# First cross attention: scores and maxima in one ring of seven PSUM banks, maxima over 512 columns, one bank for the sums

## The reference

```python
def _L0_xattn_ref(qkv, y):          # qkv: layernorm(x), (1, 256, 512); y: ctx_2048, (1, 4096, 512)
    bs, width, length = qkv.shape
    ch = width // 16                # 16 heads of 16 channels
    q = qkv.reshape(bs * 16, ch, length)
    k = v = y.reshape(bs * 16, ch, -1)          # 8192 keys a head
    scale = 1.0 / math.sqrt(math.sqrt(ch))
    weight = jnp.einsum('bct,bcs->bts', q * scale, k * scale)
    weight = jax.nn.softmax(weight.astype(jnp.float32), axis=-1)
    a = jnp.einsum('bts,bcs->bct', weight, v)
    return a.reshape(bs, -1, length)
```

## Time and profile before

| | us |
|---|---|
| median of 3 runs | 1421.54 (1421.36 to 1424.01) |
| span of the profiled execution | 1419.4 |
| first pre-score to the end of the stage | about 20 to 685 |
| stretch 325.32 to 642.54: TensorE, VectorE, ScalarE busy | 317.22, 313.66, 283.53 |
| whole span: TensorE, VectorE, ScalarE busy | 1368.0, 1153.8, 940.2 |

### The profile page before, as it was taken

The page is one execution under the profiler, slowest core; times in us unless marked ns, Lnnn a source line. Parts: engine busy times, 40 slices in busy tenths (PEclk is TensorE's granted clock), DMA queues, the critical chain, the costliest instruction groups (busy, mean ns, idle before and its releaser), DMA issues. The chain is left out here.

```text
span 1419.4 us, 27290 instructions
## 1 busy us (share of the span) xinstructions
PE 1368.0 (96%) x10665; PEld 832.0 (59%) x10665; DVE 1153.8 (81%) x1680; ACT 940.2 (66%) x1765; POOL 138.5 (10%) x171
## 2 busy tenths in 40 slices
PE   3999999999999999999898999999989989999998
PEld 2433333333333333333457999999978864567997
DVE  5999999999999999998477766666657756887665
ACT  1588888888888888889275555555434631785553
POOL 4122221211222221111000000000000000000000
PEclk9999999999999999999999999999999999999999
DMA  7545555565354554455202854555528524203751
GB/s 179 139 100 122 141 131 139 145 156 118 100 124 100 126 118 98 91 84 83 90 1 106 326 179 177 180 185 194 195 86 344 238 82 156 67 1 92 206 189 38
DMA packets 63569, 192.54 MB, mean 136 GB/s; under 512 B 32872, under 2 KB 33296, under 8 KB 51280
## 3 DMA queue, kind: packets, MB, share of 16 engines
q1 hardware_dynamic: 63264, 190.80, 47.4%
q10 hardware_dynamic: 192, 0.20, 0.1%
HBM read 165.72 MB, written 21.83 MB: 132 GB/s over the span
## 5 line engine op out<-in xcount | busy, mean ns | idle before, releaser
L530 DVE TENSOR_REDUCE pm<-bank 128x1 f32<-128x1024 f32 x512 | 621.0, 1221 | 15.9 <-PE bank L611 10.2
L589 ACT ACTIVATE probs<-bank 128x512 f32<-128x512 f32 x1024 | 554.3, 598 | 98.6 <-PE bank L630 92.9
L611 PE MATMUL bank<-kst,qst 48*128 48x512 f32 x1024 | 371.0, 452 | 21.7 <-DMA qst<-qsplit 20.0
L630 PE MATMUL bank<-qst,kst 52*128 52x512 f32 (+1 forms) x1024 | 372.4, 448 | 2.4 <-DMA qst<-nscratch 1.0
L647 PE MATMUL bank<-probs,vext 128*32 128x256 f32 x3968 | 316.7, 391 | 0.0
L630 PEld LDWEIGHTS bank<-qst,kst 52*128 52x128 f32 (+1 forms) x1024 | 153.0, 185 | 211.9 <-ACT probs L589 182.2
L1378 PE MATMUL bank<-e_xhi,e_hi 128*128 128x256 f32 (+1 forms) x768 | 217.4, 283 | 0.5 <-DVE e_xlo L1438 0.5
L1378 PE MATMUL bank<-e_xhi,e_lo 128*128 128x256 f32 (+1 forms) x768 | 217.2, 283 | 0.0
L1378 PE MATMUL bank<-e_xlo,e_hi 128*128 128x256 f32 (+1 forms) x768 | 217.2, 283 | 0.0
L647 PEld LDWEIGHTS bank<-probs,vext 128*32 128x32 f32 x3968 | 78.1, 108 | 181.1 <-ACT probs L589 91.5
L611 PEld LDWEIGHTS bank<-kst,qst 48*128 48x128 f32 x1024 | 149.8, 186 | 29.3 <-DMA qst<-qsplit 20.0
(11 more groups left out here) (233 smaller groups left out, 1515.6 us busy)
## 6 DMA issues: line engine op xcount, KB each, us to landing
raw<-wall SPq DMA_DIRECT2D x43, 1536.0 KB, 6.6
kst<-kscratch SPq DMA_DIRECT2D x192, 128.0 KB, 4.4
kscratch<-ksplit SPq DMA_DIRECT2D x15, 1024.0 KB, 4.7
kraw<-ctx_rows SPq DMA_DIRECT2D x16, 512.0 KB, 6.1
vraw<-ctx_vt SPq DMA_DIRECT2D x16, 512.0 KB, 7.2
ctxT<-ctxT SPq DMA_DIRECT2D x8, 1024.0 KB, 11.8
nat<-ctx_chunks SPq DMA_DIRECT2D x6, 1024.0 KB, 22.0
weights<-wscratch SPq DMA_DIRECT2D x16, 256.0 KB, 3.4
```

What stands on the lines that cost most here:

```text
L530: nc.vector.tensor_reduce(pm[:, h % 2, r % 4, c:c + 1], bank[:, 2 * (r % 2):2 * (r % 2) + 2, :], AX.XY, ALU.max).then_inc(pre_reduced, 1)
L589: nc.scalar.activation(probs[:, (XST * k + n) % PR, :], bank[:, S_BANK[k][n], :], ACT.Exp, scale=XSCALE).then_inc(probs_ready, 1)
L611: ins = nc.tensor.matmul(bank[:, 2 * (r % 2) + j, :], qst[64 * j:64 * j + KR, h, tt * P:tt * P + P], kst[64 * j:64 * j + KR, h % 2, c * 51 ...
L630: nc.tensor.matmul(bank[:, S_BANK[k][n], :], kst[64 * j:64 * j + rows, h % 2, m * P:m * P + P], qst[64 * j:64 * j + rows, h, :], start=Tru ...
```

## The change

Scores and pre-scores share banks 0 to 6. Slot 2s of the ring is score s, slot 2s + 1 the pre-score that is issued with it, and slot i takes bank i mod 7. So score s waits for the maximum of the pre-score issued with score s - 4, and a pre-score issued with score s for the exponential of score s - 3. The first 48 pre-scores (AHEAD, 24 steps instead of 23 ahead of the first score) still come in pairs in banks 0 to 5 with one maximum over 1024 columns; all others are reduced one by one over 512 columns, so `pm` has twice the places. The last 48 scores, which have no pre-scores beside them, use the five banks LATE_RING. The sums have bank 7 in all rounds: the first sums of each round wait for `o_copied` of the round before. The order of work within a step is as before; tiles are numbered with an offset of two, and the three half groups of sums left at the start of the last round stand in one piece.

```diff
-LAGP = 7
-PVLAG = 2
-FIRST_V = LAGP + 1 + PVLAG
-V_SCORE = 2 * (FIRST_V - LAGP) + 2
-VLAG = 2
...
+ITEMS = XN * XST
+AHEAD = XST + XP
+RING = 7
+STEP = 2
+V_BANK = 7
+V_STEP = 3
+VLAG = 2
+LATE = ITEMS - AHEAD
+LATE_RING = (6, 0, 1, 4, 5)
+PM = 8
...
+def maxima(p):
+    return p // 2 if p <= AHEAD else p - AHEAD // 2
+
+
+def score_bank(s):
+    return 2 * s % RING if s < LATE else LATE_RING[(s - LATE) % len(LATE_RING)]
+
+
+def pre_bank(p):
+    return p % 6 if p < AHEAD else (2 * (p - AHEAD) + 1) % RING
...
+            def tile_max(p):
+
+                dve.wait_ge(pre_scores, maxima(p) + 1)
+                nc.vector.tensor_reduce(max_at(p, 1), bank[:, pre_bank(p), :], AX.X, ALU.max).then_inc(pre_reduced, 1)
...
-                    if n == V_SCORE - 3 and k > 0:
+                    if k > 0 and n == (V_STEP * STEP - 1 if k < XN - 1 else 3):
                         copy_o(k - 1)
...
+                if 6 <= p < AHEAD and p % 2 == 0:
+                    pe.wait_ge(pre_reduced, maxima(p) - 2)
+                elif p >= AHEAD + 3:
+                    pe.wait_ge(probs_ready, p - AHEAD - 2)
...
+                if s < 3:
+                    pe.wait_ge(pre_reduced, maxima(AHEAD) - 2 + s)
+                elif 4 <= s < LATE + 4:
+                    tile_free(s + AHEAD - 4)
+                if LATE <= s < LATE + 4:
+                    pe.wait_ge(probs_ready, s - 3)
+                elif s > LATE + 4:
+                    pe.wait_ge(probs_ready, s - 4)
...
+            def pv(k, q, lo, hi):
+                if lo == 0:
+                    pe.wait_ge(probs_ready, XST * k + 4 * q + 4)
+                    if q == 0 and k % NS == 0:
+                        pe.wait_ge(v_ready, k // NS + 1)
+                    if q == 0 and k > 0:
                         pe.wait_ge(o_copied, k)
...
+            for i in range(AHEAD // 2):
+                pre(2 * i)
+                pre(2 * i + 1)
+                if i >= FIRST_BUSY:
                     first_busy(3)
             pe.wait_ge(const_set, 4)
+            done = 0
             for k in range(XN - 1):
...
+                for i, (first, size) in enumerate(STEPS):
+                    for n in range(first, first + size):
+                        s = XST * k + n
+                        score(s)
+                        if s < LATE:
+                            pre(s + AHEAD)
...
-            last = XN - 1
-            pe.wait_ge(pre_reduced, XP * XN)
-            for i in range(LAGP):
-                for e in range(2):
-                    late_score(last, 2 * i + e)
-                late_values(last, i)
+            last = XST * (XN - 1)
+            rest = D * XG * (XN - 1)
             for q in range(XG + VLAG):
```

More of the change, by code:

```diff
@@ L40 @@
 Q_ROWS = [(0, 0), (XC, 0), (2 * XC, 1)]
-LAGP = 7
-PVLAG = 2
-FIRST_V = LAGP + 1 + PVLAG
-V_SCORE = 2 * (FIRST_V - LAGP) + 2
-VLAG = 2
 FIRST_BUSY = 4
 DLAG = 3
[L49 to L67, removed]
+ITEMS = XN * XST
[8 more added lines that the diff above has]
+PM = 8
+SIZES = [STEP] * (XST // STEP)
+STEPS = [(sum(SIZES[:i]), n) for i, n in enumerate(SIZES)]
+def maxima(p):
[4 more added lines that the diff above has]
+    return p % 6 if p < AHEAD else (2 * (p - AHEAD) + 1) % RING
 class Count:
@@ L570, in copy_o @@
                     act.wait_ge(o_stored[h % 2], h // 2 * 16)
-                nc.scalar.copy(osb[:, 0 if half == 0 else 1 + h % 2, :], bank[:, V_BANK[k], :]).then_inc(o_copied, 1)
+                nc.scalar.copy(osb[:, 0 if half == 0 else 1 + h % 2, :], bank[:, V_BANK, :]).then_inc(o_copied, 1)
             act.wait_ge(g.ident_ready, 2)
@@ new lines, in score @@
+                if LATE <= s < LATE + 4:
+                    pe.wait_ge(probs_ready, s - 3)
+                elif s > LATE + 4:
+                    pe.wait_ge(probs_ready, s - 4)
+                nc.tensor.matmul(bank[:, score_bank(s), :], kst[64 * j:64 * j + rows, h % 2, m * P:m * P + P],
+                                 qst[64 * j:64 * j + rows, h, :], start=True, stop=True).then_inc(scores, 1)
+            def pv(k, q, lo, hi):
[4 more added lines that the diff above has]
+                    if q == 0 and k > 0:
+                        pe.wait_ge(o_copied, k)
@@ L645, in pv @@
                 for e in range(4):
                     n = XST * k + 4 * q + e
-                    ins = nc.tensor.matmul(bank[32 * e:32 * e + 32, V_BANK[k], cols], vext[:, k // NS % 2, chunk(n % XT), :], probs[:, n % PR, cols],
-                                           start=q == 0 and half == 0, stop=q == XG - 1 and half == 1)
-                if half == 1:
+                    ins = nc.tensor.matmul(bank[32 * e:32 * e + 32, V_BANK, lo:hi], vext[:, k // NS % 2, chunk(n % XT), :], probs[:, n % PR, lo:hi],
+                                           start=q == 0 and lo == 0, stop=q == XG - 1 and hi == D)
@@ L650, in pv @@
+                if hi == D:
                     ins.then_inc(pv_done, 1)
[L652 to L655, removed]
-                    ins = nc.tensor.matmul(bank[32 * e:32 * e + 32, V_BANK[k], :], vext[:, k // NS % 2, chunk(n % XT), :], probs[:, n % PR, :],
-                                           start=q == 0, stop=q == XG - 1)
-                ins.then_inc(pv_done, 1)
-            def late_score(k, n):
-                s = n - 2 * LAGP
-                if s >= 0:
-                    score(k, s)
-                elif k > 0:
-                    score(k - 1, XST + s)
```

113 lines of the change are left out of this document (47 added, 66 removed).

## The result

The changed kernel takes 1439.07 us, the median of four runs (1433.76 to 1443.58), the kernel before 1421.49 beside it: 1.0112 times as long, 95% interval [1.0079, 1.0145]. In a second comparison five runs gave 1439.82 (1434.74 to 1441.07), 1.0123 times [1.0106, 1.0140]. So it is slower, as forecast, but by 17.6 us and not by 5.6, and outside the range given (1419.5 to 1431).

What follows compares the result with a forecast made beforehand. The prediction took TensorE to bound the rounds, at 1.24 us a step. Its terms 7.3 + 0.3 - 1.7 - 0.3 gave +5.6 us, so a median of 1427.1 us, range 1419.5 to 1431.

Steps and rivals of the forecast that it cites:

- Part 1: VectorE in the rounds: maxima over 512 columns start 0.60 us apart, a round 19.5 us against TensorE's 19.82; cost 0.
- the cover that the forecast had: VectorE's 0.3 us to spare in each round, 19.5 us against 19.82 of TensorE.
- Rival (a): VectorE becomes the bound in the rounds, from 0.617 us a maximum: 1440 at 0.63, 1496 at 0.69; chance 0.08.
- Part 2: One ring of seven banks in the rounds: nothing waits, a step stays at 1.24 us with waits on all four loads.
- Rival (b): Waits on all loads shorten some 488 steps by 0.01 us each: -4.9, so 1422.2, no change; chance 0.11.
- Part 3: New sums wait for ScalarE's copy, 0.245 us in each of 30 rounds: +7.3; a step of 1.23 becomes 1.24: +0.3.
- Rival (c): No stall, the copy being over when sums come: 1419.8, or 1414.9 with shorter steps; chance 0.12, 0.07 of it with those.
- Parts 4 and 5: End of pre-scores: no drain, eight light steps of 1.00 us, -1.7; last round: earlier copy, sums at 5.7 us, -0.3.
- Part 6: Start: first score still waits for a DMA until 48.2, TensorE stands about 2 us, clock effect taken as 0.
- The signs named: Page after: sums idle about 0.24 us 30 to 31 times, rounds 20.07 apart, first score at 48.2, no end wait.

Runs made afterwards that it cites:

- a_swap: Changed kernel's 512-column maxima, work order and end, but the banks of the kernel before, with the sums' bank changing each round: 1421.58 us, 0.9997 times before.
- b_one_bank: Kernel before with one bank for the sums of all rounds, the first sums awaiting the copy, and nothing else of the change: 1433.54 us.
- a_one_wait: Changed kernel with the start filled as in a_busy and the first sums' wait for the exponentials dropped in most rounds: 1426.05 us.
- a_busy: Changed kernel with eight more pairs of matmuls that nobody reads ahead of the first score, filling TensorE's idle time: 1429.77 us, 1.0053 times before.
- b_idle2: Kernel before with the matmuls that nobody reads left out of the last two of seven steps ahead of the first score, adding idle time: 1431.81 us.
- a_one_wait_all: Changed kernel with the start filled; in every round but the first the sums' first load waits for the copy alone, the values' wait moved to ScalarE: 1427.94 us.

## Why the forecast was right or wrong, point by point

- **Part 1, smaller maxima, 0: right.** In the changed kernel VectorE runs maxima with work waiting 0.607 us apart by the events (0.60 forecast). VectorE also waits for TensorE in the changed kernel: of the 18.7 us on L539's line 10.1 fall into the round at half clock, and the other 8.5 come once a round, some 0.28 us, which is about the cover that the forecast had. Through the steady rounds each maximum is over at least 0.47 us before the score that asks for it is loaded, worked out from the events. And a_swap kept 19.8 us a round. Rival (a) is out. By the formula of the Trainium skill's page "VectorE: DVE Perf Modes", section on the TRN2 errata, they would have started 658 ns apart, an estimate from that page; the runs show 607, so the measurement decides for the shorter time, as the row did for 1024 columns.
- **Part 2, the ring, 0: right.** Steps outside the stall take 1.24 us with all four loads waiting. b_one_bank has the same rounds of 20.17 without the ring of seven. Rival (b) named steps of 1.23 us; they exist, in every second round of a_one_wait, but not in the changed kernel.
- **Part 3, one bank, +7.3 and +0.3: the mechanism right, the size too small.** The stall belongs to the one bank (b_one_bank). The mis-sized term is what a wait that ends adds, taken as 0.05 us from a VectorE row. That is right for a load with one wait: by a_one_wait its stall costs 0.243. But one or two other waits stand on the same load, and the forecast counted them as nothing; they add 0.09. So it is 30 x 0.334 = 10.0 in place of 7.3. Rival (c), no stall, is out: it came 30 times.
- **Parts 4 and 5, -1.7 and -0.3: right.** The round with the light steps takes 18.24 us in place of 19.61, with 0.33 of stall in it: -1.7. The last round to the end of the stage takes 23.31 in place of 23.58: -0.27.
- **Part 6, the start, 0: wrong, and the largest error.** This is the step that failed and put the time outside the range. The forecast saw that TensorE would stand 2 us in place of 1.05, said that no row priced this for the clock, and put it at 0 without a reason. The runs showed that this idle time halves the clock (a_busy and b_idle2), for 27.3 and 13.6 us in two executions of the changed kernel: 11.1 us in the profiled one and 9.3 in the medians. The range and the rivals got nothing for it either, though a warning was at hand: the trace of before has a stretch at half clock (684.0 to 690.8), and a round at half clock had to be far longer.
- **The sum.** With the stall at 0.334 it is 10.0 + 0.3 - 1.7 - 0.3 = 8.3 us. a_busy, the change without its effect on the clock, measures 7.9 (1429.77 - 1421.84). The 12.0 us that the forecast of +5.6 fell short are 2.7 of stall and 9.3 of clock; that this adds up to the measured 17.6 is no further check, since the 9.3 is itself the difference between the result and a_busy. The direction was forecast for a reason that holds: without the clock the change is slower by 7.9 us, and the stall is why.
- **The signs named** did their work: "the first score still at 48.2" held, "idle time 30 to 31 times about 0.24" and "rounds 20.07 apart" showed 30, 0.26 and 20.17. None of them would have shown the clock; the one line of granted clock on the page did.

## What to carry to other kernels

An edit that lets an engine finish early ahead of a fixed wait isn't free if that engine is TensorE: look at the granted clock behind the wait, fill the gap with matmuls that nobody reads, and where a forecast can't price the clock, give it a rival with the price of a stretch at half clock. A wait that stalls TensorE cost more here where other waits, long met, stood on the same weight load (0.334 us in place of 0.243); drop those that the last one implies. And a resource that alternates (here the bank of the sums) can be there so that a slow reader is off the path: taking it away cost its reader's full lateness in every round.

## What the runs showed of the hardware that I had not expected

- The clock stayed at half for 27.3, 17.1 and 13.6 us around or after idle times of 2.14, 0.63 + 1.15 and 0.92 us, with TensorE busy for 26.6, 17.1 and 13.6 of them; after 1.05 us in the kernel before it didn't fall.
- At half clock a step of scores and sums takes 2.16 us for 1.24, which is 1.74 times and not twice as long.
- One program runs the same steps at 1.227 or 1.240 us (1% apart) in alternate rounds (a_one_wait). There the short ones follow the stall with one wait, but such a stall alone doesn't bring them (a_one_wait_all). The cause is open.
- A met wait beside the one that stalls costs 0.09 us on TensorE: 51 ns for an instruction of its own, the rest around it.
- The first score, which waits for a DMA, came at 48.3 in one execution of the changed kernel and at 47.6 in another.
